# A matrix product with row normalisation on one core: three late weight tiles, a tail with the GpSimd, and three reshaped transfers

## The reference

```python
entities = jnp.einsum('be,le->bl', entity_idxs, W)
s = jnp.sum(entity_idxs, axis=1)
s_safe = jnp.where(s != 0, s, 1.0)
scale = jnp.where(s != 0, 1.0 / s_safe, 1.0)
return entities * scale[:, None]
```

## Time and profile before

| what | us |
|---|---|
| median of the runs | 147.88 |
| the profiled execution, its own time | 147.88 |
| span of the profiled execution | 146.1 |
| PE busy in the span | 135.2 |
| DVE busy | 83.3 |
| ACT busy | 67.3 |
| HBM read 57.60 MB | 398 GB/s over the span |

### The profile page before, as it was taken

One profiled execution on the slowest core, in us unless ns is written; L12 is line 12 of the kernel. 1 busy time (PEld: TensorE's weight loads), 2 busy tenths in 40 slices (PEclk: granted clock), 3 DMA queues, 4 the chain that ended last, 5 costly groups with the idle time before them and its releaser, 6 DMA issues.

```text
span 146.1 us, 2413 instructions
## 1 busy us (share of the span) xinstructions
PE 135.2 (93%) x785; PEld 77.3 (53%) x785; DVE 83.3 (57%) x165; ACT 67.3 (46%) x152; POOL 0.5 (0%) x10
## 2 busy tenths in 40 slices
PE   0588999989999999989999999999999999999990
PEld 0223565545555556645555565565556655655550
DVE  0197615609726496461479645566381836666694
ACT  3195513508505474351367434455360725455582
POOL 1000000000000000000000000000000000000000
PEclk9999999999999999999999999999999999999999
DMA  5999999999999999999999999999999999999922
GB/s 150 403 428 435 428 459 409 418 454 414 419 449 405 421 428 449 419 439 434 420 424 428 428 419 428 424 416 421 426 421 426 421 414 408 414 410 400 359 89 72
DMA packets 7303, 58.18 MB, mean 398 GB/s; under 512 B 814, under 2 KB 1582, under 8 KB 3842
## 3 DMA queue, kind: packets, MB, share of 16 engines
q1 hardware_dynamic: 7298, 58.13, 95.5%
HBM read 57.60 MB, written 0.52 MB: 398 GB/s over the span
## 4 chain that ended last, share of the span: by engine, by line
PE 44%; DMA 43%; SPq 6%; DVE 3%; issue 2%; POOLq 0%; DVEq 0%
PE acc L447 44%; DMA xw<-loop 33%; DMA x_final<-ends 10%; SPq L224 4%; SPq L222 1%; DVE dve_out L343 1%; DVE y_sum L395 1%; DVE row_sum L389 1%; DVE row_sum L392 0%; SPq L213 0%; SPq L214 0%; DVE any_low L426 0%; PE acc L489 0%; DVE inexact L428 0%; POOLq L209 0%
## 5 line engine op out<-in xcount | busy, mean ns | idle before, releaser
L447 PE MATMUL acc<-parts,xw 128*128 128x385 bf16 x720 | 121.6, 332 | 2.1 <-POOLq L209 1.7
L447 PEld LDWEIGHTS acc<-parts,xw 128*128 128x128 bf16 x720 | 70.5, 99 | 53.5 <-POOLq L209 5.5
L332 DVE TENSOR_TENSOR w_rest<-xw 128x384 f32<-128x384 f32 x30 | 16.7, 558 | 51.2 <-POOLq L209 51.2
L276 ACT ACTIVATE parts<-xw 128x384 bf16<-128x384 bf16 x30 | 15.8, 525 | 63.9 <-POOLq L209 63.8
L343 DVE SCALAR_TENSOR_TENSOR dve_out<-xw 128x1152 bf16<-128x1152 uint16 x30 | 40.5, 1351 | 0.0
L283 ACT ACTIVATE act_out<-xw 128x768 bf16<-128x768 uint16 x30 | 24.8, 827 | 0.0
L338 DVE TENSOR_TENSOR parts<-w_rest 128x384 bf16<-128x384 f32 x31 | 17.4, 560 | 1.5
L279 ACT ACTIVATE parts<-w_rest 128x384 bf16<-128x384 bf16 x31 | 16.3, 527 | 4.0 <-DVE w_rest L332 2.7
L447 PE MATMUL acc<-parts_short,xw_short 84*128 84x385 bf16 x8 | 2.7, 522 | 5.1 <-ACT parts_short L279 5.1
L283 ACT ACTIVATION_READ_ACCUMULATOR act_out<-xw x30 | 5.6, 186 | 0.0
L447 PE MATMUL acc<-parts_alone,x_final 128*128 128x385 bf16 x24 | 5.2, 327 | 0.0
(11 more groups left out here) (40 smaller groups left out, 17.1 us busy)
## 6 DMA issues: line engine op xcount, KB each, us to landing
xw<-loop SPq DMA_DIRECT2D x9, 2304.0 KB, 18.5
xw<-loop SPq DMA_DIRECT2D x10, 1728.0 KB, 19.2
xw<-loop SPq DMA_DIRECT2D x8, 1152.0 KB, 18.4
xw<-loop SPq DMA_DIRECT2D x8, 576.0 KB, 19.2
x_final<-ends SPq DMA_DIRECT2D x7, 384.0 KB, 15.3
xw_head<-ends SPq DMA_DIRECT2D x1, 960.0 KB, 6.1
out<-y SPq DMA_DIRECT2D x3, 128.0 KB, 1.7
xw_short<-ends SPq DMA_DIRECT2D x1, 378.0 KB
```

What stands on the lines that cost most here:

```text
L276: nc.scalar.activation(parts[0:rows, :, 0:L], top(words), ACT.Copy)
L332: nc.vector.tensor_tensor(tiles(w_rest[0:rows, buf, 0:n * L], n), words, top(words), ALU.subtract).then_inc(rest_done, 1)
L447: return nc.tensor.matmul(acc[:, b, 0:N], x, parts, start=first, stop=last)
```

## The change

Four edits.

1. The three `ALONE` weight tiles leave the head transfer (1,920 words a row become 1,536) and get a transfer of their own, `w_alone`, issued right behind piece 27 (the piece with tile 82). ACT and DVE split it after unit 27, with semaphores of its own. For that, the last of the 5 rounds is written out behind the loop on both engines; on DVE the first round, which was written out before, goes into the loop. TensorE waits for the two new semaphores before its last six tiles.
2. In the tail POOL multiplies banks 0 to 3 (two pairs), ACT only banks 4 to 6. DVE adds up fewer low halves: checks 0 and 1 as before, a quarter of check 2, and none of checks 3 to 5, which ACT takes whole. SP waits for POOL's semaphore in front of the first two outputs.
3. Piece 5 (tiles 18 to 21) is issued as three transfers of 112, 8 and 8 rows; POOL waits for all three.
4. The short tile is loaded as 96 rows. The 12 rows more are bytes that follow in the same tensor, and nothing reads them.

The diff, cut to its core (the semaphores' declarations, the slow path and the packing on the host are left out):

```diff
@@ transfers
+UNEVEN = 5
+GROUPS = (0, P - 16, P - 8, P)
+POOL_PAIRS = 2
+ALONE_BEHIND = 27
-    shapes = [(P, B + (1 + UNIT + ALONE) * L), (short, B + L)]
+    shapes = [(P, B + (1 + UNIT) * L), (short, B + L), (P, ALONE * L)]
+    SHORT_ROWS = -(-short // 16) * 16
+        def row_groups(k):
+            return tuple(zip(GROUPS, GROUPS[1:])) if k == UNEVEN else ((0, P),)
-            sp.dma_start(xw_short[0:short, :], edge(1)).then_inc(short_in, 16)
+            sp.dma_start(xw_short[0:SHORT_ROWS, :], short_rows).then_inc(short_in, 16)
...
-                sp.dma_start(xw[:, j:j + n, :], piece(k)).then_inc(piece_in[k], 16)
+                for r0, r1 in row_groups(k):
+                    sp.dma_start(xw[r0:r1, j:j + n, :], piece(k)[r0:r1, :, :]).then_inc(piece_in[k], 16)
+                if k == ALONE_BEHIND:
+                    sp.dma_start(w_alone[:, :], edge(2)).then_inc(alone_in, 16)
...
-            for b0, b1 in PAIRS:
-                if b1 < BANKS:
-                    sp.wait_ge(y_ready, b1)
+            for pair, (b0, b1) in enumerate(PAIRS):
+                if pair < POOL_PAIRS:
+                    sp.wait_ge(y_pool_ready, b1)
+                elif b1 < BANKS:
+                    sp.wait_ge(y_ready, b1 - PAIRS[POOL_PAIRS][0])
@@ gpsimd
+            for pair in range(POOL_PAIRS):
+                pool.wait_ge(inverse_done, pair + 1)
+                pool.wait_ge(y_summed, pair + 1)
+                for b in range(*PAIRS[pair]):
+                    nc.gpsimd.tensor_scalar(y[:, b, :], y_sum[:, b, :], row_sum[:, b, 1:2], None,
+                                            ALU.mult).then_inc(y_pool_ready, 1)
@@ scalar
-            split(tiles(w_alone, ALONE), parts_alone, ALONE, ALONE_REST, ALONE_SPLIT)
-            with act.Fori(0, ROUNDS) as i:
+            with act.Fori(0, ROUNDS - 1) as i:
...
+            for s in range(SLOTS):
+                unit(ROUNDS - 1, s)
+                if s == ALONE_SLOT:
+                    act.wait_ge(alone_in, 16)
+                    top_part(tiles(w_alone, ALONE), parts_alone)
+                    act.wait_ge(alone_rest_done, 1)
+                    mid_part(parts_alone, ALONE, ALONE_REST).then_inc(alone_top_parts_done, 1)
-            scale(0)
             check(2)
-            scale(1)
@@ vector
         def dve_share(c):
-            return last_words(c).shape[1] // 2
+            return last_words(c).shape[1] // (2 if c + 1 < DVE_CHECKS else 4) if c < DVE_CHECKS else 0
...
-            for s in range(SLOTS):
-                unit(0, s)
-            with dve.Fori(1, ROUNDS) as i:
+            with dve.Fori(0, ROUNDS - 1) as i:
                 for s in range(SLOTS):
                     unit(i, s)
+            for s in range(SLOTS):
+                unit(ROUNDS - 1, s)
+                if s == ALONE_SLOT:
+                    dve.wait_ge(alone_in, 16)
+                    rest_of(tiles(w_alone, ALONE), ALONE, ALONE_REST).then_inc(alone_rest_done, 1)
+                    dve.wait_ge(alone_rest_done, 1)
+                    lo_part(parts_alone, ALONE, ALONE_REST).then_inc(alone_lo_done, 1)
...
             finish(1)
-            check(3)
-            check(4)
             finish(2)
-            check(5)
             finish(3)
@@ tensor
+            pe.wait_ge(alone_top_parts_done, 1)
+            pe.wait_ge(alone_lo_done, 1)
```

More of the change, by code:

```diff
@@ L73, in edge @@
         return ends[at:at + rows * cols].rearrange("(p f) -> p f", p=rows)
+    short_rows = ends[table[1][0]:table[1][0] + SHORT_ROWS * ROW].rearrange("(p f) -> p f", p=SHORT_ROWS)
     def piece(k):
@@ L87, in rec_kernel @@
         xw = sb("xw", [P, RING, ROW], F32)
-        xw_head = sb("xw_head", [P, B + (1 + UNIT + ALONE) * L], F32)
+        xw_head = sb("xw_head", [P, B + (1 + UNIT) * L], F32)
         xw_short = sb("xw_short", [P, ROW], F32)
+        w_alone = sb("w_alone", [P, ALONE * L], F32)
         x_final = sb("x_final", [P, BANKS, LAST, P], F32)
@@ L274, in _, with top_part, mid_part @@
         def _(act):
+            def top_part(words, parts, rows=P):
+                nc.scalar.activation(parts[0:rows, :, 0:L], top(words), ACT.Copy)
+            def mid_part(parts, n, buf, rows=P):
+                rest = top(tiles(w_rest[0:rows, buf, 0:n * L], n))
+                return nc.scalar.activation(parts[0:rows, :, L:2 * L], rest, ACT.Copy)
             def split(words, parts, n, buf, count, rows=P):
-                nc.scalar.activation(parts[0:rows, :, 0:L], top(words), ACT.Copy)
+                top_part(words, parts, rows)
                 act.wait_ge(rest_done, count)
-                rest = top(tiles(w_rest[0:rows, buf, 0:n * L], n))
-                nc.scalar.activation(parts[0:rows, :, L:2 * L], rest, ACT.Copy).then_inc(top_parts_done, 1)
+                mid_part(parts, n, buf, rows).then_inc(top_parts_done, 1)
             def low_sum(words, col, buf, rows=P):
@@ L294, in _, with unit @@
             low_sum(tiles(xw_head[:, DVE_WORDS:B], 1), 0, 0).then_inc(act_checked, 1)
-            with act.Fori(0, ROUNDS) as i:
-                for s in range(SLOTS):
[L297 to L302, removed]
+            def unit(i, s):
+                u = SLOTS * i + s
+                act.wait_ge(slot_in[UNIT * s + UNIT - 1], i + 1)
+                act.wait_ge(products_done, used(u + 1 - SLOTS))
+                split(unit_w(s), parts[:, (s + 1) % SLOTS, :, :], UNIT, (s + 1) % 2, unit_split(u + 1))
+                act.wait_ge(act_checked, used(u - 2))
+                low_sum(unit_x(s, DVE_WORDS), u + 2, (s + 1) % 2).then_inc(act_checked, 1)
+            with act.Fori(0, ROUNDS - 1) as i:
+                for s in range(SLOTS):
+                    unit(i, s)
+            for s in range(SLOTS):
[5 more added lines that the diff above has]
+                    mid_part(parts_alone, ALONE, ALONE_REST).then_inc(alone_top_parts_done, 1)
             def check(c):
@@ L537 @@
         at += n
-    ends = [side_by_side([head_x, head_w], w_tiles[:UNIT], last_w[:ALONE]), np.concatenate([x_t[:short], w_t[:short]], axis=1)]
+    ends = [side_by_side([head_x, head_w], w_tiles[:UNIT]), np.concatenate([x_t[:short], w_t[:short]], axis=1),
+            side_by_side(last_w[:ALONE])]
     for b, j0, j1 in FINAL:
```

40 lines of the change are left out of this document (22 added, 18 removed).

## The result

The changed kernel takes 156.26 us (median of 4 runs, 156.05 to 156.38) against 147.97 us for the kernel before (4 runs, 147.88 to 148.25): 1.0558 times as long, interval 1.0540 to 1.0575. The forecast was 146.8 us and the range ended at 148.2. The profiled execution took 156.05 us with a span of 154.2 us, so the 8.1 us stand in the trace. Two runs lie apart from the others of their kernel and are left out of the ratios, though not of the medians: 156.52 us of `p112_16` and 205.01 us of `oldtail` (granted clock 0.67); neither has an explanation.

A forecast was written before the change was run, and what follows sets the result against it. The stream bounds the kernel until tile 44 lands (74.03 us), then TensorE. TensorE's end -1.08 and tail -0.1 make -1.18, less some hundredths for added transfers: -1.1 from 147.88, so 146.8 us, range 146.5 to 148.2.

The forecast's parts named there:

- the piece in three: Piece 5's loading: 112, 8 and 8 rows relieve the late engine of one row; -0.69 us taken, bounds -0.69 to +0.69.
- the third bound: Piece 5's loading: the latest engine is among the eight loaded with 9 rows, +0.69 us.
- The unevenness: Piece 5's rows: 9 on eight engines, 7 on the others; the late engine is relieved, -0.69 us.
- rival A: Piece 5: one late engine is relieved, another is among the loaded eight, so no gain; 147.4 us, chance 0.22.
- The head and the three late tiles: Weight loads: a smaller head starts TensorE's run at tile 44 0.455 us earlier; margin at tile 89 limits it to 0.395.
- The short tile: Short tile's load: 12 rows more, 0 us taken, upper bound 0.13 us; packets under 512 B rise to 848.
- The tail: Behind TensorE's end: DVE's last reduction starts earlier, last multiply 0.15 us earlier, of which 0.1 us is kept.
- rival D: Tail: POOL's multiplies take above 1.7 us and hold up SP's outputs; near 150 us, chance 0.04.
- Rival C: Written-out round: instruction packets at about 105 us delay TensorE; 147.4 us, or 148.7 if the latest engine is loaded; chance 0.10.
- The forecast's own tests: Chain goes over to TensorE at 73.0 us if right, 73.6 under rival A, 74.3 if the latest engine is loaded.

The follow-up runs named there:

- p112_16: The changed kernel with piece 5 cut into 112 and 16 rows: 154.73 us, 1.0405 of the kernel before.
- oldtail: `whole_84` with the tail of the kernel before, the moved weights kept: 148.23 us, 1.0011 of the kernel before.
- extra_adjacent: `whole` plus two added transfers of 8 neighbouring rows of piece 5 into words nobody reads: 153.38 us, 1.0366 of the kernel before.
- p64_64: The changed kernel with piece 5 cut into rows 0 to 63 and 64 to 127: 155.66 us, 1.0509 of the kernel before.
- even_odd: The changed kernel with piece 5 cut into its even and its odd rows, 64 each: 147.66 us, 0.9977 of the kernel before.
- strided_uneven: The changed kernel with piece 5 in five groups of spread rows, still 9 rows on eight engines and 7 on eight: 149.57 us, 1.0096 of the kernel before.
- one_tile_uneven: Like `strided_uneven`, but only tile 21 in spread groups, tiles 18 to 20 as one 128-row transfer: 148.12 us, 1.0006 of the kernel before.
- whole: The changed kernel with piece 5 in one transfer of 128 rows, other three edits kept: 147.69 us, 0.9984 of the kernel before.
- before_96: The kernel before with only the short tile loaded as 96 rows: 147.94 us, 1.0001 of the kernel before.
- whole_84: `whole` with the short tile of 84 rows again: 147.61 us, 0.9978 of the kernel before.

## Why the prediction was wrong

It was wrong in one step, and by sign and size: **the piece in three**. The step priced a row at 0.69 us of one engine, whatever transfer it is in, and looked only at how many rows each engine gets; its bounds, -0.69 and +0.69 us, were that price times one row. The price came from 128-row transfers, whose rows lie on all partitions. In a transfer on neighbouring partitions alone the row is slower (1.10 us and more for each of the 80 packets between 34 and 42 us), and the rows of other transfers with it: two transfers of 8 rows cost 5.7 us (`extra_adjacent`), a piece in two halves of 64 rows takes twice as long (`p64_64`), and even and odd rows cost nothing (`even_odd`). "On even engines this only costs", the step said; beyond the row it counted some hundredths for two semaphore writes.

The trace of before had no transfer on a few partitions of the ring, so it could not bound this price. The prediction named a rule that speaks against disjoint halves, and then cut it down to "a small loss, which is the third bound without its mechanism". That was the mistake that could have been avoided. The rule as the Trainium skill gives it there (DMA: Bandwidth & Descriptors, rules for kernel authors: same engines, hence serial) would indeed cost little, and `even_odd` bears that out. The rule that fits the runs is the one on ports in the Trainium skill (SBUF — State Buffer, Door 1), which the prediction didn't weigh. It should have stood as a rival near 153 us, an estimate from that section: 147.4 and two transfers of 2.7 us.

The other steps:

- **The unevenness** (-0.69 us as taken). Not seen: `strided_uneven` and `one_tile_uneven` give no gain. The packets' records suggest why, though no view prints it: followed from packet to packet, the 16 KB instruction packet sits on an engine that is relieved, and an 8 KB one on an engine that is loaded, which then is last. That is rival A's mechanism. It is read from one profiled execution of each kernel, and the slow packets that are left are mixed into the times, so it is likely and not shown. The even share of 9 and 7 rows itself is: eight engines carry 49 large packets and eight 47.
- **The head and the three late tiles** (-0.395 us). In `whole` TensorE's run starts at 73.78 against 74.13, 0.35 us earlier where 0.455 was forecast, and takes 68.55 us against 68.43, the 0.12 us being mostly its wait at tile 89, where the forecast put it (0.06 us). It ends 0.23 us earlier. The mechanism held; the start's term was 0.1 us too large. Tile 44's landing differs by up to 0.2 us between kernels with the same head (74.03 before, 74.25 in `before_96`), so the rest stays open.
- **The short tile** (0). Right, and so were the packets: 848 under 512 B, 34 more.
- **The tail** (-0.1 us). Right: 0.15 us shorter, and ACT's operation of 1152 words is 1.17 us, as forecast. POOL's multiplies, for which no row stood, take 603 ns in `whole` and 649 in the changed kernel, above the 0.4 us taken and far below the 1.7 us from which they would count (rival D):

```profile
L239 POOL TENSOR_SCALAR y<-y_sum,row_sum 128x128 f32<-128x128 f32 x4 | 2.6, 649 | 146.4 <-DVE row_sum L445 146.4
```

- **Without the piece**, the prediction's terms give 147.88 - 0.395 - 0.1 = 147.4 us; `whole` measured 147.69. Rival C did not happen: behind tile 44 TensorE has no wait longer than that at tile 89.
- **The forecast's own tests** answered at once: the chain went over at 82.2 us, not 73.0, 73.6 or 74.3, so none of the cases written down was the true one.

The best versions are those without the contiguous cut: `even_odd` (0.9977), `whole_84` (0.9978) and `whole` (0.9984). All are ahead of the kernel before by 0.2 to 0.3 us, less than the 0.3% that was set as the bound for no change.

## What to carry to other kernels

When a stream of full transfers runs beside it, don't cut a transfer into runs of neighbouring partitions: such a part slows the other packets too for as long as it is in flight. Pieces of fewer tiles on all 128 partitions keep the stream's rate here (414 GB/s in the second stretch of the earlier trace rows), and so do even and odd rows (425 GB/s); five interleaved groups cost 1.9 us. Price a new shape of transfer by the partitions it touches and not by its rows per engine, and if the trace has no such shape, give its bound the width that this ignorance deserves. Look at the rate beside the DMA share: here the share was about 1.00 at 430 GB/s and at 147.

## What the runs showed of the hardware

- A transfer of 8 neighbouring partitions, 147 KB, costs the whole stream 2.8 us; of 8 partitions four apart, 0.9 us; its bytes are 0.34 us. Transfers on all 128 partitions are held up with it, those behind it and, on the engine that is late, those ahead of it (`extra_adjacent`: piece 5 lands at 43.05 us and not at 37.91).
- 112 neighbouring rows are slow too. The rate is 258 GB/s between 30 and 38 us, the first stretch of the cut piece, and the rest of 16 rows as one transfer (`p112_16`) instead of two saves only 1.5 us by the medians (2.3 by the ratios). By the rule of the Trainium skill (SBUF — State Buffer, Door 1) 112 rows reach all 16 ports and should be nearly free, so this part of the loss has no shown cause.
- What a stall of TensorE costs beyond its length depends on what it meets next. In `p64_64` it stood 4.3 us, starts at 45.54 at the lower clock (0.82 of full speed granted on the mean of 46 to 60 us) with products 0.32 us apart, and never waits again; its chain has one run to the end, where `whole`'s rate of 68.55 / 416 = 0.165 us a product would make it 102.8 us:

```profile
19.65 25.79 DMA xw<-loop
...
45.54 105.18 PE acc L497 x624
```

The 2.4 us more are what 15 products at half speed cost. TensorE ends at 150.7 us. An estimate: had it been at full speed, it would have waited for the stream again and ended about 1.2 us earlier, since tile 44 lands at 80.94 us by the transfers' records and 416 products take 68.5.
